# A routed and graph network of eight layers on one core: fifth tile earlier, next matrices into used places, additions between the gelu sums

## The chip, the cores and the metric

The kernel runs on one core of a Trainium2 chip, in one launch. The metric is the time of one execution on the device, in microseconds (us); the time before is the median of three runs.

The core has five engines, each with its own in-order instruction stream: TensorE (PE; PEld is its weight loading), VectorE (DVE), ScalarE (ACT), GpSimd (POOL) and SyncE (SP), which here only issues transfers. They wait for one another on semaphores. TensorE writes into PSUM, eight banks of 512 fp32 values a partition.

## The reference, cut to what matters

`x` has 625 rows of 512 values. Eight layers are added to it one after another, each on a layer-normed `x`; the change touches the third to the seventh.

```
x = x + L0_gnn(ln(x)); x = x + L0_ffn(ln(x))
x = x + L1_gnn(ln(x))     # first graph network in the names below
x = x + L1_ffn(ln(x))     # first expert layer
x = x + L2_gnn(ln(x))     # second graph network, 3 layers
x = x + L2_ffn(ln(x))     # second expert layer
x = x + L3_gnn(ln(x), noise)   # four attention blocks
x = x + L3_ffn(ln(x))     # routed experts
```

The end of L1_gnn, for each row: `h = rowsum @ W1 + b1`, `h = relu(layernorm(h) * gamma + beta)` with 128 values, and `relu(h @ W2 + b2)` with 512, divided by a row weight, is added to `x`.

L2_gnn repeats three times: `agg = CNT @ x`, `y = agg @ Wtop[i] + edge part @ Wbot[i] + bs[i]`, `x = relu(layernorm(x + y) * gamma + beta)`.

L2_ffn is a mixture of 8 experts in which every expert sees every row:

```
top_p = normalized two largest softmax(x @ Wg)
for i in range(2):
    h = gelu((x * top_p[i]) @ W1 + b1)     # 512 x 512 over all experts
    out = out + h @ W2 + sum_e b2
```

L3_gnn begins with a layer norm whose gain and offset are `cond @ s1_w + s1_b` and `cond @ b1_w + b1_b` with 16 values of `cond` a row, made from the noise.

## The kernel before, in words

The 625 rows are five tiles of P = 125 rows (`NT = 5`); `X[:, t, :]` is the residual stream. Each layer is written out by hand for every engine in the order in which it is to be issued; nothing plans it. PSUM is given out by `Slots`: two one-bank slots `T` (turned, that is transposed, rows), two two-bank slots `W` and two one-bank slots `N`. Each engine calls `next` or `skip` in the same sequence; a slot has a semaphore `filled` and one `taken`, and TensorE fills a slot only when what it held two uses before is taken.

**Matrices.** `WR` holds two sets of three 512 x 512 matrices, `wm(s, j)`. `loads` (line 483) is SyncE's program. `load` (line 491) issues a batch after `weights_used` has reached the number of batches that TensorE is through with; TensorE counts it with `weights_done` (line 710), a drain. For the second graph network set 0 holds Wtop of its three layers and set 1 the small Wlast. Behind it, lines 605 to 639, comes the batch of the second expert layer (f_W1, f_W2, f_b2; lines 605 and 498), which waits for the end of the third layer. After it SyncE writes zeros into `x_slots` (4.25 MB, from the cleared tile MODW, lines 618 to 622), waits for their landing, loads eight pieces of modulation weights (modw, line 608), the attention biases (line 612), and the qkv matrices (line 635, issued at line 498).

**First graph network.** Per tile: `hidden_of` (line 1101) makes h in an `N` slot; VectorE's `hidden` (line 2527) adds b1 and takes statistics, POOL takes the inverse root (line 1942), `hidden_normed` (line 2540) normalizes; TensorE turns it (`turn_hidden`, line 1105), ScalarE applies relu; `second` (line 1111) multiplies by W2 in an `N` slot after a product with one row of ones for the bias (line 1113); ScalarE's `second` (line 1747) applies relu; VectorE's `added` (line 2545) adds. VectorE takes tile 4's hidden rows (line 2562) after `added(0)`. Since `N` has two slots, the second product of tile 1 uses the bank that held h of tile 4.

**Second graph network.** Per layer, lines 1168 to 1193: an aggregation of five parts, one for each tile of normed rows, and five narrow products, one for each tile.

**Second expert layer.** TensorE, lines 1215 to 1255: turn each tile, its routing logits (`logit`, into one slot), and its inner projection with f_W1 (tiles 0, 1 and 4 in `N`, line 724; tiles 2 and 3 in one `W` slot, line 1210). Then `modulation(t)` (line 1020), the turn of the gelu sum and `second_of_two(t)` (line 1233: a bias product with eight rows, line 1235, then f_W2, line 1238) for each tile. ScalarE: the five copies of turned rows, rounding of `cond` into CONDR (line 1804), rounding of modw into MODR (`round_weights`, line 1808), the exponential of the routing (`router_exp`, line 1690), then for each tile two gelus (`inner`), the copy of the turned sum and of the modulation. VectorE: the logits' copy and maxima (lines 2680, 2683), the two shares, then the loop at line 2716: two scaled inputs (`hidden_inputs`, line 2696), `split_condition` (line 2706) behind the first tile's and `split_weights` (line 2713) behind the second's, and the sum of the two gelus one tile later (line 2728). When all five sums are made, `three(streamed, stream_normed, modulated_norm)` (line 2783) adds the second products to X (line 2123), normalizes twice and applies the modulation.

Of the kernel before, what the change touches and what calls it, by code (L numbers as in the profile page):

```python
# [21 lines left out]
N, E, D = 625, 10000, 512  # L22
P, NT = 125, 5
# [161 lines left out]
def program(nc, a, out, loops):  # L185
# [11 lines left out]
    def sem(name):  # L197
        return ctx.enter_context(nc.semaphore(name))
# [8 lines left out]
    with ctx:  # L207
# [169 lines left out]
        GE = [[view(PT_ + 512 * (2 * b + i), P, D) for i in range(2)] for b in range(2)]  # L377
        EMN = view(V_ + 1265, 64, N)
# [71 lines left out]
        cond_rounded, cond_split = sem("cond_rounded"), sem("cond_split")  # L450
        mod_rounded, mod_split = sem("mod_rounded"), sem("mod_split")
# [31 lines left out]
        def loads(sp):  # L483
# [121 lines left out]
            load([mat(0, 0, "f_W1"), mat(0, 1, "f_W2"), (WR[0:8, 0, 2, 0:D], a["f_b2"])])  # L605
# [16 lines left out]
            sp.dma_start(x_slots[2048:2048 + 128, :], MODW[:, 0, :]).then_inc(slots_zeroed, 16)  # L622
            sp.wait_ge(slots_zeroed, 16 * 5)
# [71 lines left out]
        def _(pe):  # L695
# [472 lines left out]
            for l in range(3):  # L1168
# [17 lines left out]
                for t in range(NT):  # L1186
                    o = fill("N")
                    mm(o.ap[0:P, :], EA2[0:65, tile(t)], WR[0:65, 1, 1, D * l:D * (l + 1)], start=True, stop=False)
                    for f in range(K4):
                        if t == 0:  # L1190
                            copied(gathered[f])
                        last = mm(o.ap[0:P, :], HT[:, f, tile(t)], wm(0, l)[:, f, :], start=False, stop=(f == K4 - 1))
                    last.then_inc(o.filled, 1)
            weights_done()
# [38 lines left out]
            def second_of_two(t, turned_inner):  # L1233
                s = fill("N")
                mm(s.ap[0:P, :], TWOS[:, :], WR[0:8, 0, 2, 0:D], start=True, stop=False)
                copied(turned_inner)
                for k in range(K4):
                    last = mm(s.ap[0:P, :], HT[:, k, tile(t)], wm(0, 1)[:, k, :], start=False, stop=(k == K4 - 1))
                last.then_inc(s.filled, 1)
# [228 lines left out]
        def _(act):  # L1468
# [334 lines left out]
            transpose_y()  # L1803
            fn(CONDR[:, :], COND4, ACT.Copy).then_inc(cond_rounded, 1)
            def round_weights(j, rows_in_):

                act.wait_ge(rows_in_, n.add(rows_in_, 64))
                fn(MODR[:, :, :], MODW[:, j:j + 2, :], ACT.Copy).then_inc(mod_rounded, 1)
# [10 lines left out]

            round_weights(0, modw_in)  # L1820
# [102 lines left out]
        def _(pool):  # L1923
# [95 lines left out]
            inverse_roots((0, 1, 2, 3, 0, 4, 1, 2, 3, 4))  # L2019
# [53 lines left out]
        def _(dve):  # L2073
# [471 lines left out]
            def added(t):  # L2545
# [12 lines left out]
            fifth = psum.next("N")  # L2558
            seconds = [psum.next("N")[0:2] for t in range(NT)]
            added(0)  # L2560
            dve.wait_ge(fifth[0].filled, fifth[1])
            v.tensor_tensor(HB[:, 4, :], fifth[0].ap[0:P, 0:128], ROWS[:, R_B1:R_B1 + 128], ALU.add)\
             .then_inc(fifth[0].taken, 1)
            dve.wait_ge(fifth[0].taken, fifth[1])
            stats(4, HB[:, 4, :])
            hidden_normed(3)
            added(1)
            norm_y(0)
            hidden_normed(4)
# [108 lines left out]
            psum.skip(T=NT)  # L2678
            s = take("W")
            v.tensor_copy(LG[:, :, :], s.ap[0:P, 0:8 * NT].rearrange("p (t e) -> p t e", t=NT)).then_inc(s.taken, 1)  # L2680
            dve.wait_ge(s.taken, n.now(s.filled))
            for t in range(NT):
                step(v.max(M8[:, t, :], LG[:, t, :]))
            softmax_of_two()
            couple = psum.next("W")

            def hidden_inputs(t):
                if t in (2, 3):
                    s = couple[0]
                    dve.wait_ge(s.filled, couple[1])  # L2690
                    rows = s.ap[0:P, D * (t - 2):D * (t - 1)]
                else:
                    s = take("N")
                    rows = s.ap[0:P, 0:D]
                for i in range(2):
                    last = v.scalar_tensor_tensor(GE[t % 2][i], rows, TW[:, t, 1 + i:2 + i],  # L2696
                                                  ROWS[:, R_FB1:R_FB1 + D], ALU.mult, ALU.add)
                    if i == 0:
                        last.then_inc(negmax_ready, 1)
                last.then_inc(negmax_ready if t == 2 else s.taken, 1)  # L2700

# [14 lines left out]
            for t in range(NT + 1):  # L2716
                if t < NT:
                    if t >= 2:
                        dve.wait_ge(y_ready, n.now(y_ready))
                    hidden_inputs(t)  # L2720
                if t == 0:
                    split_condition()
                if t == 1:
                    split_weights(0)
                if t:
                    dve.wait_ge(exp_ready, n.add(exp_ready, 2))
                    n.add(y_ready)
                    v.tensor_tensor(Y[0:P, t - 1, :], GE[(t - 1) % 2][0], GE[(t - 1) % 2][1], ALU.add)\
                     .then_inc(y_ready, 1)
# [53 lines left out]
            three(streamed, stream_normed, modulated_norm)  # L2783
# [241 lines left out]
```

## Time and profile before

| | |
|---|---|
| median of 3 runs | 2321.89 us |
| lowest, highest | 2321.63, 2322.45 us |
| span of the profiled execution | 2314.6 us (no other time is given for it) |
| TensorE busy | 2155.4 us, 93% |
| VectorE, ScalarE, GpSimd busy | 1043.3, 729.8, 540.3 us |
| chain that ended last | PE 68%, DVE 11%, issue 8%, PEld 4%, ACT 3%, DMA 3%, POOL 3% |

Times in the profile are in us from the start of the span. A row of the timeline is: start, duration, engine, line, operation, what is written from what, shapes, count, and in brackets how long the engine was idle before it and what ended that. In the chain of waits a piece is start, duration and what; "issue" is time in which the engine waited for nothing that the profile shows. In the table of windows the columns are the window, its length, then busy time and number of instructions of PE, PEld, DVE, ACT and POOL, the granted TensorE clock as a share of 2.4 GHz, the share of the DMA engines and GB/s. A busy TensorE is not a TensorE at its peak, and the recorded ends of its products overlap a little with the next.

### The profile page before, as it was taken

Reading aid. Unit: us, or ns where it says so; the run is one execution under the profiler, and the core shown is the slowest. Engines: PE = TensorE matmul, PEld = TensorE weight load, DVE = VectorE, ACT = ScalarE, POOL = GpSimd, SP = SyncE. Lnnn points to the kernel's source line nnn. Section 1 sums busy time; section 2 is a strip of 40 time slices with the busy share of each in tenths; the row PEclk is TensorE's granted clock in tenths of the full one; section 3 lists DMA queues with packets and bytes.
Section 4 is the critical chain, followed back from the end, with each engine's and each line's share of the span. In section 5 each row is a group of like instructions: output and inputs, shape, how many; then the busy total and the mean of one; then the engine's idle time right before and its main releaser. Section 6 shows DMA issues by size and latency. Waiting matters only on the chain.

```text
span 2314.6 us, 21913 instructions
## 1 busy us (share of the span) xinstructions
PE 2155.4 (93%) x8137; PEld 1248.1 (54%) x8137; DVE 1043.3 (45%) x2156; ACT 729.8 (32%) x1221; POOL 540.3 (23%) x457
## 2 busy tenths in 40 slices
PE   6899896888889999988999999999999999999998
PEld 3566563787445555444565565565555544444443
DVE  8897677886324332454454453453453410000002
ACT  1576555675421110003243243243242111111110
POOL 4677762332210000110202202202202200022202
PEclk9999998787999979998999999999999899999999
DMA  9522205431020110023101101101101577787832
GB/s 344 167 31 38 27 4 126 123 78 58 0 96 19 55 55 7 1 76 116 65 9 59 64 10 59 65 10 59 55 1 55 195 272 297 296 306 294 298 143 71
DMA packets 61507, 237.47 MB, mean 103 GB/s; under 512 B 23343, under 2 KB 28419, under 8 KB 39276
## 3 DMA queue, kind: packets, MB, share of 16 engines
q1 hardware_dynamic: 31898, 168.25, 20.3%
q0 software_dynamic: 26336, 62.19, 8.8%
q10 hardware_dynamic: 3168, 5.63, 0.7%
q8 instruction: 66, 1.08, 0.2%
q14 instruction: 39, 0.32, 0.0%
HBM read 204.06 MB, written 31.96 MB: 102 GB/s over the span
## 4 chain that ended last, share of the span: by engine, by line
PE 68%; DVE 11%; issue 8%; PEld 4%; ACT 3%; DMA 3%; POOL 3%; SPq 0%; PEldq 0%; ACTq 0%; DVEq 0%; POOLq 0%
PE PS L996 10%; PE PS L724 10%; PE PS L717 7%; PE PS L1387 7%; PE PS L1396 7%; PE PS L1425 6%; PE PS L868 3%; PE PS L1293 3%; PE PS L1034 2%; PE PS L1273 2%; PE PS L735 1%; DMA pair_scores<-TS,SIDX 1%; PEld PS L717 1%; DVE AR L2406 1%; POOL pair_scores L1971 1%
## 5 line engine op out<-in xcount | busy, mean ns | idle before, releaser
L1942 POOL TENSOR_TENSOR RSTD<-VE,HALF 125x1 f32<-125x1 f32 x100 | 81.7, 817 | 1017.3 <-DVE VE L2101 1017.3
L996 PE MATMUL PS<-XT,WR 128*128 128x500 f32 (+2 forms) x992 | 236.2, 396 | 8.4 <-ACT XT L1493 4.4
L868 PE MATMUL PS<-HR,HOT 125*125 125x512 f32 x800 | 212.8, 414 | 16.4 <-DVE HOT L2245 16.4
L724 PE MATMUL PS<-WR,XT 128*125 128x512 f32 (+1 forms) x464 | 208.0, 596 | 12.2 <-DVE AR L2696 7.7
L2911 DVE TENSOR_TENSOR AR<-AR,PS 128x512 f32<-128x512 f32 (+1 forms) x44 | 30.2, 687 | 404.9 <-PE PS L1396 404.9
L996 PEld LDWEIGHTS PS<-XT,WR 128*128 128x128 f32 x992 | 146.0, 194 | 89.2 <-issue 74.7
L868 PEld LDWEIGHTS PS<-HR,HOT 125*125 125x125 f32 x800 | 147.9, 193 | 58.5 <-DVE HOT L2245 16.8
L1960 POOL DMA_INDIRECT pair_sums<-CW,SIDX x80 | 136.2, 1703 | 56.3 <-DMA pair_sums<-CW,SIDX 24.5
L724 PEld LDWEIGHTS PS<-WR,XT 128*125 128x125 f32 x464 | 87.1, 194 | 101.4 <-issue 86.4
L717 PE MATMUL PS<-XT,WR 128*128 128x113 f32 (+3 forms) x432 | 127.5, 453 | 1.8 <-DVE CW L2209 1.3
L1902 ACT ACTIVATE AR<-PS 128x512 f32<-128x512 f32 (+1 forms) x44 | 26.3, 597 | 299.3 <-PE PS L1387 299.3
L2123 DVE TENSOR_TENSOR AR<-PS,AR 125x512 f32<-125x512 f32 x55 | 38.0, 691 | 178.7 <-PE PS L724 106.3
L717 PEld LDWEIGHTS PS<-XT,WR 128*128 128x128 f32 (+1 forms) x432 | 69.8, 196 | 65.3 <-issue 64.1
L1971 POOL DMA_INDIRECT pair_scores<-TS,SIDX x80 | 89.1, 1114 | 61.4 <-DMA pair_scores<-TS,SIDX 46.5
L1493 ACT ACTIVATE XT<-PS 128x500 f32<-128x500 f32 x60 | 35.4, 590 | 214.0 <-PE PS L735 214.0
L717 PE MATMUL PS<-AR 128*125 128x113 f32 (+3 forms) x360 | 102.4, 439 | 0.0
L1425 PE MATMUL PS<-AR,MODW 128*128 128x512 f32 (+1 forms) x192 | 86.4, 593 | 0.7 <-ACT MODW L1891 0.7
L1994 POOL TENSOR_TENSOR AR<-AR,CNT 125x625 f32<-125x625 f32 x40 | 56.8, 1419 | 104.9 <-ACT AR L1658 104.9
L717 PEld LDWEIGHTS PS<-AR 128*125 128x125 f32 (+1 forms) x360 | 57.3, 187 | 43.8 <-issue 43.6
L724 PE MATMUL PS<-WR,AR 128*125 128x512 f32 (+1 forms) x200 | 76.6, 530 | 1.7 <-ACT AR L1876 0.9
L2245 DVE SCALAR_TENSOR_TENSOR HOT<-AR,NODE,WR 125x500 fp32r<-125x500 int16 x100 | 71.2, 731 | 7.0 <-ACT WR L1525 6.0
L2266 DVE TENSOR_REDUCE TS<-WR 125x8 f32<-125x512 f32 x80 | 54.4, 680 | 42.1 <-DMA pair_scores<-TS,SIDX 42.1
(422 smaller groups left out, 3940.3 us busy)
## 6 DMA issues: line engine op xcount, KB each, us to landing
WR<-in_qkv SPq DMA_DIRECT2D x12, 1024.0 KB
WR<-in_omm SPq DMA_DIRECT2D x12, 1024.0 KB
pair_scores<-CNT SPq DMA_DIRECT2D x1, 12212.0 KB, 36.4
AR<-pair_scores SPq DMA_DIRECT2D x5, 2187.5 KB
AR<-in_x_a SPq DMA_DIRECT2D x10, 1024.0 KB, 9.8
AR<-in_x_b SPq DMA_DIRECT2D x10, 1024.0 KB, 4.9
AR<-in_x_c SPq DMA_DIRECT2D x10, 1024.0 KB, 7.2
WR<-in_x_a SPq DMA_DIRECT2D x8, 1024.0 KB, 8.9
```

What stands on the lines that cost most here:

```text
L717: last = mm(s.ap[0:parts, c0:c1], lhs(k), rhs(k)[:, c0:c1], start=(k == 0), stop=(k == terms - 1))
L724: last = mm(s.ap[0:P, 0:cols], lhs, rhs, start=(k == 0), stop=(k == len(pairs) - 1))
L868: last = mm(DIFF[m % 4], HOT[g % 2][0:P, k, tile(j)], HR[0:P, k, :, b, :], start=(k == 0 and b == 0), stop=(k == NT - 1 and b == 1))
L996: last = mm(by_tile(s)[:, t0:t1, :], w[:, k, 128 * m:128 * (m + 1)], XT[:, k, P * t0:P * t1].rearrange("p (c n) -> p c n", n=P), start=(k ...
L1293: one = mm(main.ap[:, 0:MAIN], v_, PTH[h % 2][:, k, 0:MAIN], start=(k == 0), stop=(k == NT - 1))
L1387: last = mm(bank(2 + k % 2, rows_of(k)), stationary(k, c), w[:, c, :], start=(c == 0), stop=(c == K4 - 1))
L1396: last = mm(bank(4 + k % 2, rows_of(k)), stationary(k, c), w[:, c, :], start=(c == 0), stop=(c == K4 - 1))
L1425: last = mm(bank(6 + n % 2, rows), HTX[k % 2][:, c, 0:rows], w[:, c, :], start=(u == 0 and c == 0), stop=((is_shared(k) or u == 1) and c = ...
L1942: g.tensor_tensor(RSTD[:, t:t + 1], VE[:, t:t + 1], HALF[:, :], ALU.pow)\
L1960: g.indirect_dma_start(out=pair_sums[m % 2], out_offset=bass.IndirectOffsetOnAxis(ap=SIDX[:, m:m + 1], axis=0), in_=CW[:, m, :], in_offset ...
L1971: g.indirect_dma_start(out=pair_scores, out_offset=bass.IndirectOffsetOnAxis(ap=SIDX[:, m:m + 1], axis=0), in_=TS[:, m % SCORES_AHEAD, :], ...
L2245: v.scalar_tensor_tensor(HOT[g % 2][0:P, k, :], IDB[g // 2 % 2][0:P, 1, 500 * (g % 2):500 * (g % 2 + 1)], NODE[:, 0, k:k + 1], FROM[q % 4] ...
```

## The change

Four edits go together. VectorE's tile 4 of the hidden rows is taken and normalized before the first addition, and POOL's roots follow that order. f_W1 and f_W2 are loaded singly into the places of Wtop 0 and Wtop 1 when TensorE is through with the layer that used them (a drain with a semaphore behind layers 0 and 1), f_b2 into a new place `OUTER_BIAS`, all behind the zeroing of `x_slots`, which so stands at the start of the second graph network. ScalarE rounds `cond` before the five turned copies instead of behind them, and VectorE splits it before the logits. VectorE's first addition of a second product stands before the last gelu sum instead of behind it; the rest of `three` is written out in the same order.

```diff
+        OUTER_BIAS = view(PT_ + 2340, 8, D)
+        graph_layer_done = sem("graph_layer_done")
@@ SyncE
-            load([mat(0, 0, "f_W1"), mat(0, 1, "f_W2"), (WR[0:8, 0, 2, 0:D], a["f_b2"])])
...
             sp.dma_start(x_slots[2048:2048 + 128, :], MODW[:, 0, :]).then_inc(slots_zeroed, 16)
+            k2 = batch[0]
+            batch[0] += 1
+            for l, (dst, src) in enumerate((mat(0, 0, "f_W1"), mat(0, 1, "f_W2"), (OUTER_BIAS, a["f_b2"]))):
+                if l < 2:
+                    sp.wait_ge(graph_layer_done, l + 1)
+                sp.dma_start(dst, src).then_inc(loaded[k2 % 2], 16)
+                landed[k2 % 2] += 16
             sp.wait_ge(slots_zeroed, 16 * 5)
@@ TensorE, behind each layer l of the second graph network
+                if l < 2:
+                    pe.drain().then_inc(graph_layer_done, 1)
...
-                mm(s.ap[0:P, :], TWOS[:, :], WR[0:8, 0, 2, 0:D], start=True, stop=False)
+                mm(s.ap[0:P, :], TWOS[:, :], OUTER_BIAS, start=True, stop=False)
@@ ScalarE
-            transpose_y()
             fn(CONDR[:, :], COND4, ACT.Copy).then_inc(cond_rounded, 1)
...
+            transpose_y()
             round_weights(0, modw_in)
@@ POOL
-            inverse_roots((0, 1, 2, 3, 0, 4, 1, 2, 3, 4))
+            inverse_roots((0, 1, 2, 3, 4, 0, 1, 2, 3, 4))
@@ VectorE, first graph network
             hidden(3)
             hidden_normed(2)
-            fifth = psum.next("N")
+            hidden(4)
+            hidden_normed(3)
+            hidden_normed(4)
             seconds = [psum.next("N")[0:2] for t in range(NT)]
             added(0)
-            dve.wait_ge(fifth[0].filled, fifth[1])
-            v.tensor_tensor(HB[:, 4, :], fifth[0].ap[0:P, 0:128], ROWS[:, R_B1:R_B1 + 128], ALU.add)\
-             .then_inc(fifth[0].taken, 1)
-            dve.wait_ge(fifth[0].taken, fifth[1])
-            stats(4, HB[:, 4, :])
-            hidden_normed(3)
             added(1)
             norm_y(0)
-            hidden_normed(4)
@@ VectorE, second expert layer
+            split_condition()
             psum.skip(T=NT)
             s = take("W")
...
+            inner_at = {t: psum.next("N") for t in (0, 1, 4)}
+            seconds = [psum.next("N") for t in range(NT)]
...
+            def second_streamed(t):
+                s, k = seconds[t][0:2]
+                dve.wait_ge(s.filled, k)
+                v.tensor_tensor(X[0:P, t, :], s.ap[0:P, :], X[0:P, t, :], ALU.add).then_inc(s.taken, 1)
+                dve.wait_ge(s.taken, k)
+                stats(t, X[0:P, t, :])
...
-            three(streamed, stream_normed, modulated_norm)
+            for t in range(NT + 1):
+                if t < NT:
+                    if t >= 2:
+                        dve.wait_ge(y_ready, n.now(y_ready))
+                    hidden_inputs(t)
+                if t == 1:
+                    split_weights(0)
+                if t == NT:
+                    second_streamed(0)
+                if t:
+                    inner_sum(t - 1)
+            for t in range(1, NT + 2):
+                if t < NT:
+                    second_streamed(t)
+                if t <= NT:
+                    stream_normed(t - 1)
+                if t >= 2:
+                    modulated_norm(t - 2)
```

## Rows read from the trace of the kernel before

**Rows 1.** The chain of waits, 1018 to 1130 us: start, us, what.
```profile
1031.66 15.82 DMA x_slots<-MODW
...
1048.43 12.51 DMA MODW<-in_modw
...
1060.96 1.06 ACT MODR L1808
...
1062.04 1.28 ACT L1692
...
1063.33 0.22 ACT TW L1692
```

**Rows 2.** SyncE's timeline, issues between 820 and 1112 us.
```profile
1028.46 0.80 SPq L498 DMA_DIRECT2D WR<-in_f_W  x2
...
1058.39 6.12 SPq L498 DMA_DIRECT2D WR<-in_qkv  x3
```

**Rows 3.** TensorE's timeline in the second expert layer.
```profile
1032.25 0.94 PE L1202 MATMUL PS<-WG,XT 128*125 128x8 f32 x8
1037.39 5.44 PE L724 MATMUL PS<-WR,XT 128*125 128x512 f32 x8 [4.20 <-DMA WR<-in_f_b]
...
1043.89 3.68 PE L724 MATMUL PS<-WR,XT 128*125 128x512 f32 x8
...
1052.14 0.59 PE L735 MATMUL PS<-CS,Y 125*128 125x125 f32 x4
...
1065.67 6.65 PE L724 MATMUL PS<-WR,XT 128*125 128x512 f32 x8 [7.69 <-DVE AR L2696]
...
1087.88 1.28 PE L1235 MATMUL PS<-WR,TWOS 8*125 8x512 f32 x2 [3.11 <-DVE X L2123]
1089.09 5.19 PE L1238 MATMUL PS<-WR,AR 128*125 128x512 f32 x8
```

**Rows 4.** VectorE's timeline in the second expert layer.
```profile
1036.60 0.54 DVE L2106 TENSOR_SCALAR Y<-X,MV,RSTD 125x512 f32<-125x512 f32 x1
...
1054.49 0.20 DVE L2680 COPY LG<-PS 125x40 f32<-125x40 f32 x1 [12.60 <-PE PS L1202]
...
1055.74 0.17 DVE L2603 TENSOR_TENSOR TW<-M 125x5 f32<-125x5 f32 x1
...
1064.21 1.41 DVE L2696 SCALAR_TENSOR_TENSOR AR<-PS,TW,AR 125x512 f32<-125x512 f32 x2
1065.65 1.62 DVE L2706 TENSOR_TENSOR CONDR<-AR,CONDR 32x625 fp32r<-32x625 f32 x2
...
1072.05 0.68 DVE L2728 TENSOR_TENSOR Y<-AR 125x512 f32<-125x512 f32 x1
...
1080.96 0.69 DVE L2728 TENSOR_TENSOR Y<-AR 125x512 f32<-125x512 f32 x1 [3.38 <-ACT AR L1796]
1086.53 0.69 DVE L2728 TENSOR_TENSOR Y<-AR 125x512 f32<-125x512 f32 x1 [4.88 <-ACT AR L1796]
```

**Rows 5.** Timelines of TensorE and VectorE, hidden rows of the first graph network.
```profile
799.33 0.35 DVE L2538 SCALAR_TENSOR_TENSOR AR<-AR,RSTD 125x128 f32<-125x128 f32 x1
...
804.36 0.28 DVE L2562 TENSOR_TENSOR AR<-PS,AR 125x128 f32<-125x128 f32 x1
...
804.70 2.06 PE L1113 MATMUL PS<-AR,ONES 1*125 1x512 f32 x2 [2.73 <-DVE AR L2562]
```

**Rows 6.** Table of windows: length, busy times, granted clock, DMA share, GB/s.
```profile
792.00:801.90 9.90, 9.75 (x55) 6.40 (x55) 5.35 (x22) 1.99 (x5) 2.30 (x4) 1.00 0.00 0
802.00:804.70 2.70, 0.00 (x0) 0.00 (x1) 1.94 (x6) 0.75 (x2) 0.17 (x1) 0.50 0.00 0
804.70:822.00 17.30, 17.30 (x22) 5.21 (x22) 8.37 (x22) 2.98 (x6) 3.30 (x5) 0.50 0.00 1
...
1072.00:1088.00 16.00, 12.89 (x44) 6.39 (x43) 6.37 (x11) 8.27 (x16) 0.00 (x0) 1.00 0.12 47
```

**Rows 7.** TensorE's timeline behind the drain that ends the first expert layer.
```profile
898.77 11.06 PE L1174 MATMUL PS<-CNT,AR 125*128 125x512 f32 x40 [0.26 <-issue]
```

More of the change, by code:

```diff
@@ L2675, in _ @@
             three(summed, lambda t: relu_normed(t, 2), norm_y)
[L2678 to L2700, printed above, removed]
             def split_condition():
@@ L2714, in split_weights @@
                                 MODR[64:128, :, :].bitcast(F32), ALU.subtract).then_inc(mod_split, 1)
[L2716 to L2729, printed above, removed]
+            split_condition()
@@ new lines, in _ @@
+            psum.skip(T=NT)
+            s = take("W")
+            v.tensor_copy(LG[:, :, :], s.ap[0:P, 0:8 * NT].rearrange("p (t e) -> p t e", t=NT)).then_inc(s.taken, 1)
+            dve.wait_ge(s.taken, n.now(s.filled))
+            for t in range(NT):
+                step(v.max(M8[:, t, :], LG[:, t, :]))
+            softmax_of_two()
+            couple = psum.next("W")
+            inner_at = {t: psum.next("N") for t in (0, 1, 4)}
+            seconds = [psum.next("N") for t in range(NT)]
@@ new lines, in hidden_inputs @@
+            def hidden_inputs(t):
+                if t in (2, 3):
+                    s, k = couple[0:2]
+                    rows = s.ap[0:P, D * (t - 2):D * (t - 1)]
+                else:
+                    s, k = inner_at[t][0:2]
+                    rows = s.ap[0:P, 0:D]
+                dve.wait_ge(s.filled, k)
+                for i in range(2):
+                    last = v.scalar_tensor_tensor(GE[t % 2][i], rows, TW[:, t, 1 + i:2 + i],
+                                                  ROWS[:, R_FB1:R_FB1 + D], ALU.mult, ALU.add)
+                    if i == 0:
+                        last.then_inc(negmax_ready, 1)
+                last.then_inc(negmax_ready if t == 2 else s.taken, 1)
@@ new lines, in inner_sum @@
+            def inner_sum(t):
+                dve.wait_ge(exp_ready, n.add(exp_ready, 2))
+                n.add(y_ready)
+                v.tensor_tensor(Y[0:P, t, :], GE[t % 2][0], GE[t % 2][1], ALU.add).then_inc(y_ready, 1)
+            def second_streamed(t):
+                s, k = seconds[t][0:2]
+                dve.wait_ge(s.filled, k)
+                v.tensor_tensor(X[0:P, t, :], s.ap[0:P, :], X[0:P, t, :], ALU.add).then_inc(s.taken, 1)
+                dve.wait_ge(s.taken, k)
+                stats(t, X[0:P, t, :])
```

## The prediction

> **What bounds the kernel now.** TensorE is busy almost everywhere, so I read the chain of waits first and looked for the pieces of it that are not TensorE. Around the second expert layer it holds two transfers and what hangs on them: 15.82 us in which the slots in memory are zeroed, then 12.51 us for the rows of the modulation weights (modw), then ScalarE's rounding of those rows, and behind it, in the same in-order engine, the exponential of the routing softmax [rows 1]. SyncE's queue shows why: it waits for the end of the second graph network before it issues f_W1 and f_W2 at 1028.46, the zeroing and the modw rows stand behind them, and the qkv weights get out only at 1058.39 [rows 2]. TensorE's timeline shows the price: 4.20 us idle for the transfer of f_b2 that closes the f batch, a projection of tile 4 that starts only at 1065.67 and takes 6.65 us where one at full clock takes 3.68, and 3.11 us idle in front of the third second product [rows 3]. One other place is touched, the hidden rows of the first graph network: 2.73 us idle for the bank of the fifth tile [rows 5]. The windows give TensorE's clock there [rows 6].
>
> **Part 1, fifth tile in front of the first addition.** VectorE now reads tile 4 out of its bank at 804.36, behind `added(0)`, though it was through with the normalization of tile 2 at 799.7 [rows 5]. The same reading then comes at about 799.7 to 800.0, and the bank is free before TensorE asks for it at 804.70 - 2.73 = 801.97. The statistics and two normalizations that come with it fill VectorE's idle time up to `added(0)`, which waits for ScalarE in both kernels. The reordered roots on POOL only follow VectorE's order. So the 2.73 us idle goes: **-2.7 us**. What is late next is TensorE itself: from 804.7 to 822 it is busy 17.30 of 17.30 us, at 1.2 GHz [rows 6]. That clock decides the size. It was full up to 801.9, during 9.75 us busy of 9.90, and half from 802.0 on, so it had gone down as the idle time began, not behind it, and 17 us of unbroken work (products with one row of ones, alternating with the W2 products) did not bring it back [rows 6]. What runs before 801.9 is unchanged, so I let the clock fall again. Lower end of the gain 2.0, upper 11.4 (rival A).
>
> The Trainium skill, "TensorE: Matmul & The Clock Gate", Part 1 and its list for kernel authors, holds that idle time throttles the array and work releases it. By that the removed stall would also give back the slow stretch behind it. The rows here speak against it, since the fall comes with no idle time ahead of it; it is rival A.
>
> **Part 2, the next matrices into used places.** Added: a drain of TensorE behind layers 0 and 1 of the second graph network. The trace has no drain inside those layers; the nearest is the one ahead of 898.77, with 0.26 us idle [rows 7]. Bounds 0.2 and 0.6 each, since weight loading can't run ahead over it either; I take 0.4, **+0.8 us** for both. VectorE's last normalization of a layer is asked for only by the last of the five parts of the next aggregation, so nothing else waits.
>
> Moved on SyncE's queue: the five zeroing transfers go right behind Wlast and the clearing of MODW, at the start of this network, where no other transfer is queued; then f_W1 after layer 0, f_W2 and f_b2 (to a new place, since its old one still holds layer 2's matrix) after layer 1, and, as the zeroing has long landed, the eight modw transfers and the attention biases. All of it comes some 40 us before layer 2 ends. The qkv load waits only for that end and issues near 1028.5 instead of 1058.39 [rows 2]; it is not needed before 1095. The queue is never late: even 13 us for the modw rows, as before [rows 1], end before 1000.
>
> What that gives, step by step. The first projection starts when the first routing logits are done, at 1032.25 + 0.94 = 1033.2, instead of 1037.39 [rows 3]. Full speed would end it at 1036.9; since TensorE has just stood idle I let half of it run at 1.2 GHz: 1038.4. Tile 2's normed rows are there at 1037.14 [rows 4], no longer the last to come. Before, from the start of the first projection to the fourth turn (1037.39 to 1052.14) it took 14.75 us; that contains 5.44 for the first projection, so 9.3 behind it, plus the 0.3 us or so of pipelining: turn of tile 4 at 1048.1 [rows 3]. From that turn to the copy of the logits VectorE needed 1054.49 - 1052.14 = 2.35 [rows 3, 4]: 1050.4. The maxima and the difference end 1.42 later (1054.49 to 1055.91 [rows 4]): 1051.9. Here, before, ScalarE stood at the modw rows and exponentiated at 1063.33 [rows 1]; now rounding (1.06) and table load (1.28) [rows 1] start at about 1049.4, end with the difference, and the exponential runs at once. From it to the first hidden input it is 1064.21 - 1063.33 = 0.9 [rows 1, 4]: 1052.8 against 1064.21, **11.4 us earlier**: 4.1 from the f weights, 7.3 from the modw rows. The projection of tile 4 follows 1.46 later (1065.67 - 1064.21), at 1054.3, with TensorE idle for under 1 us instead of 7.7, so at full clock: 3.68 instead of 6.65, end 1057.9 against 1072.3. That is 14.4.
>
> What is late next: the second gelu sum. It ended at 1072.05 + 0.68, 8.52 behind the first hidden input; `split_condition` (1.62 us of VectorE between the two [rows 4]) is moved ahead of the logits, where VectorE idled for 12 us, and ScalarE's copy for it to before the turns: 6.9. So it ends at 1059.7, where TensorE would turn that tile at 58.8: 0.9 back. **-13.5 us** for the part; if the first projection runs at full clock -15.2, if the clock stays low for one more projection -10.
>
> **Part 3, additions between the gelu sums.** The third second product waits until `streamed(0)` has emptied its bank, and VectorE does that only behind the last gelu sum, which itself waited for ScalarE until 1086.53 [rows 4]. Now it stands in front of that sum: right behind the fourth (1080.96 + 0.69 = 1081.65 [rows 4]), 3 us before TensorE asks at 1087.88 - 3.11 = 1084.77 [rows 3]. So 3.11 idle goes, and with it the slow clock behind it: 5.19 against 3.68, and some 0.2 in the bias product ahead of it, 4.8 in all. The next bank is freed by the addition of tile 1, right behind the last sum at 87.2, in time. I give back 0.2 since the first modulated rows of tile 0 come out level with TensorE's turn of them. VectorE's tail behind the last product is the same work. **-4.6 us**; bounds -3 (VectorE late) and -4.8.
>
> Sum: -2.7 + 0.8 - 13.5 - 4.6 = **-20.0 us**. The profiled execution has a span of 2314.6; the page gives no separate time for it, and the median of 2321.89 lies 7.3 above the span, which I carry over unchanged. 2321.9 - 20.0 = **2301.9 us**. Everything behind the layer is shifted as it is; only the clock's falls and returns in it may land elsewhere, for which I allow 2 us either way.
>
> **Rivals.**
> A: the clock stays at 2.4 GHz in the hidden rows. For: the stall that is removed stands at the head of the slow stretch. Against: the fall came with none ahead of it [rows 6]. Price: half of 17.3 us, 8.7 more gain: **2293.2**. Chance 0.13.
> B: the clock stays low from the first f projection to that of tile 4. For: in the hidden rows busy TensorE stayed at 1.2 GHz. Against: in the kernel before the same projections took 5.44 and then 3.68, so it returned inside one [rows 3], and 1072 to 1088 ran at 1.00 [rows 6]. Price: four projections of 3.68 doubled, 14.7: gain 5.3, **2316.6**. Chance 0.06.
> C, the other side: with nothing waited for any more, the mixture of eight-row bias products, turns and ten groups of 3.68 keeps TensorE at 1.2 GHz through the whole layer. Price 10 x 3.68 = 36.8 against 20.0: **2338.7**, slower; it decides from more than five of the ten groups at half clock. For: as B, and 1-row products did it at 804.7. Against: rows 6 again. Chance 0.02.
> D: the early transfers change nothing, because something else holds the exponential (the turn of tile 4 is late). Then only parts 1 and 3 and the end of the cold projection stay, about 9 us: **2313**. Against: ScalarE's only recorded wait there is for modw [rows 1]. Chance 0.05.
>
> **How the numbers follow.** Forecast 0.74; A, B, C, D as given. The forecast's own range is 2297 to 2307. To leave out no more than 2 in 10 with its ends and A's uncertain place, the range is 2291 to 2309. A difference of 0.2% (4.6 us) is about what can be told from none here. Faster by more than that: all but C and a sliver of B and D: 0.97; within 0.01; slower 0.02.
>
> **What would show it.** No idle at L1113 and its pair still near 4.1 us: part 1 as forecast; at 2.1 us, A. The zeroing within the first layer of the second graph network, an f matrix behind each of the first two layers, qkv at the end of the third: the queue. MODR rounded by ScalarE directly behind the last turn's copy, and 3.7 us for all narrow projections but the first: part 2. No idle over 0.5 us at L1235: part 3. Gaps above 1 us behind layers 0 and 1 would refute the price of the drains. A total above 2309 would mean that a wait which I have not seen replaced the modw rows.

## The result and the profile after

The changed kernel took 2298.51 us (median of 4, 2295.84 to 2299.26) against 2321.76 before (median of 4); the ratio is 0.9908 with a 95% interval of 0.9884 to 0.9932, that is 16 to 27 us less. The profiled execution had a span of 2293.7 us, 20.9 less than before.

| | before | after |
|---|---|---|
| median | 2321.76 | 2298.51 |
| span of the profiled execution | 2314.6 | 2293.7 |
| TensorE busy | 2155.4, 93% | 2152.0, 94% |
| VectorE, ScalarE, GpSimd busy | 1043.3, 729.8, 540.3 | 1043.4, 729.8, 537.8 |

The work is the same; what went is time in which TensorE waited, or worked at 1.2 GHz. The change adds and moves lines. TensorE's L743 is the old L735 (turns), L732 the old L724, L1121 and L1123 the old L1113 and L1115, L1212 the old L1202, L1245 and L1248 the old L1235 and L1238. VectorE's L2701 is the old L2680 (copy of the logits), L2609 the old L2603, L2719 the old L2696 (hidden inputs), L2688 the old L2706 (split of `cond`); the gelu sum has L2728 in both.

SyncE's timeline of the changed kernel (it answers [rows 2]):

```profile
895.06 0.33 SPq L500 DMA_DIRECT2D WR<-in_Wlast  x1
900.46 3.06 SPq L621 DMA_DIRECT2D x_slots<-MODW  x4
...
938.69 43.96 SPq L629 DMA_DIRECT2D WR<-in_f_W  x2
982.68 0.33 SPq L629 DMA_DIRECT2D AR<-in_f_b  x1
983.06 6.76 SPq L609 DMA_DIRECT2D MODW<-in_modw  x8
...
1026.06 1.30 SPq L500 DMA_DIRECT2D WR<-in_qkv  x3
...
1084.59 1.28 SPq L500 DMA_DIRECT2D WR<-in_omm  x3
```

The zeroing goes out at 900.5, f_W1 after the first layer, f_W2, f_b2 and the modulation rows after the second, qkv at 1026, the end of the third. Before, all of these were issued between 1028.5 and 1058.4. (A duration such as 43.96 contains the wait between the first and the last of the merged issues.)

ScalarE's and VectorE's timelines in the second expert layer (they answer [rows 1, 4]):

```profile
1046.31 1.05 ACT L1818 ACTIVATE MODR<-MODW 128x1024 fp32r<-128x1024 f32 x1
1047.38 1.28 ACT L1702 ACT_TABLE_LOAD   x1
1049.00 0.21 ACT L1702 ACTIVATE TW<-TW 125x5 f32<-125x5 f32 x1 [0.34 <-DVE TW L2609]
```

```profile
1034.08 0.54 DVE L2117 TENSOR_SCALAR Y<-X,MV,RSTD 125x512 f32<-125x512 f32 x1
...
1039.40 1.62 DVE L2688 TENSOR_TENSOR CONDR<-AR,CONDR 32x625 fp32r<-32x625 f32 x2
1047.55 0.20 DVE L2701 COPY LG<-PS 125x40 f32<-125x40 f32 x1 [6.53 <-PE PS L1212]
...
1048.80 0.17 DVE L2609 TENSOR_TENSOR TW<-M 125x5 f32<-125x5 f32 x1
...
1049.89 2.73 DVE L2719 SCALAR_TENSOR_TENSOR AR<-PS,TW,AR 125x512 f32<-125x512 f32 x4
...
1055.95 0.68 DVE L2728 TENSOR_TENSOR Y<-AR 125x512 f32<-125x512 f32 x1
...
1064.72 0.69 DVE L2728 TENSOR_TENSOR Y<-AR 125x512 f32<-125x512 f32 x1 [4.41 <-ACT AR L1806]
1065.33 0.68 DVE L2733 TENSOR_TENSOR X<-PS,X 125x512 f32<-125x512 f32 x1
...
1070.29 0.69 DVE L2728 TENSOR_TENSOR Y<-AR 125x512 f32<-125x512 f32 x1 [3.14 <-ACT AR L1806]
```

ScalarE rounds the modulation rows directly behind its last copy and loads its table, and the exponential waits 0.34 us for VectorE, not 7 us for a transfer. The split of `cond` fills idle time ahead of the logits. The first addition (1065.33) stands between the fourth gelu sum (1064.72) and the last (1070.29).

TensorE's timeline there (it answers [rows 3]):

```profile
1029.72 1.13 PE L1212 MATMUL PS<-WG,XT 128*125 128x8 f32 x8
1030.71 5.18 PE L732 MATMUL PS<-WR,XT 128*125 128x512 f32 x8
...
1036.95 3.68 PE L732 MATMUL PS<-WR,XT 128*125 128x512 f32 x8
...
1045.20 0.59 PE L743 MATMUL PS<-CS,Y 125*128 125x125 f32 x4
...
1051.35 3.70 PE L732 MATMUL PS<-WR,XT 128*125 128x512 f32 x8 [0.31 <-DVE AR L2719]
...
1056.78 0.62 PE L743 MATMUL PS<-CS,Y 125*128 125x125 f32 x4 [0.84 <-DVE Y L2728]
...
1068.46 1.12 PE L1245 MATMUL PS<-AR,TWOS 8*125 8x512 f32 x2
1069.51 3.70 PE L1248 MATMUL PS<-WR,AR 128*125 128x512 f32 x8
```

The first projection follows the logits at once, and is slow (5.18 for 3.68) as it was before; the projection of tile 4 takes 3.70 instead of 6.65; a new wait of 0.84 stands at the second turned sum (L743 at 1056.78); and no idle time is left at L1245, and the product behind it (L1248) takes 3.70 instead of 5.19.

TensorE's timeline and the table of windows at the hidden rows of the first graph network ([rows 5, 6]), and TensorE's timeline behind the first new drain ([rows 7]):

```profile
801.52 1.98 PE L1121 MATMUL PS<-AR,ONES 1*125 1x512 f32 x2
803.43 2.07 PE L1123 MATMUL PS<-WR,AR 128*125 128x512 f32 x2
```

```profile
791.70:801.50 9.80, 9.73 (x55) 6.40 (x55) 7.37 (x30) 1.90 (x5) 2.89 (x5) 1.00 0.00 0
801.60:819.00 17.40, 17.14 (x22) 5.13 (x23) 8.25 (x19) 3.97 (x9) 2.89 (x4) 0.50 0.00 0
...
1051.00:1088.00 37.00, 32.98 (x97) 15.06 (x96) 27.48 (x56) 14.19 (x27) 6.19 (x8) 1.00 0.06 22
```

```profile
938.87 11.06 PE L1182 MATMUL PS<-CNT,AR 125*128 125x512 f32 x40 [0.26 <-issue]
```

The stall of 2.73 is gone. What follows is as before: 17.14 us busy of 17.40, at 1.2 GHz. The clock is low from the second pair of products on, though TensorE was busy 9.73 of the 9.80 us ahead of it and nothing stalls in between.

### A measure that is finer than the runs

Executions of the same kernel differed by up to 18 us (58 runs of the kernel before: 2310.23 to 2328.71), and most of that seems to arise ahead of 770 us, where the change does nothing: the first product of the aggregation in the first graph network started between 763.2 and 777.2 in the 14 profiles. From there on profiles of the same code agree to a fraction of a microsecond, except where TensorE's clock falls or returns at another product (1.3 to 1.7 us at a time in the table), so each kernel is read between landmarks, all starts of TensorE instructions: A that aggregation (L1092 before), B the first aggregation of the second graph network, C the first turn behind it, D the first modulation of the second expert layer, E the first bias product there (L1235 before), F the first product of the attention blocks (L996 at 1112.42 before). One profile each, in us:

| kernel | A to B | B to C | C to D | D to E | E to F | F to end |
|---|---|---|---|---|---|---|
| before | 129.20 | 129.99 | 43.00 | 1.81 | 38.85 | 1202.18 |
| changed | 126.06 | 130.98 | 28.25 | 2.85 | 34.19 | 1202.18 |
| e1 fifth only | 124.74 | 129.99 | 41.55 | 3.18 | 42.06 | 1202.71 |
| e2 transfers only | 129.04 | 130.99 | 29.94 | 2.84 | 41.97 | 1202.62 |
| e3 additions only | 129.13 | 129.99 | 42.84 | 2.03 | 34.17 | 1202.63 |
| e4 bias 125 rows | 114.51 | 130.98 | 28.27 | 2.84 | 34.17 | 1202.72 |
| e5 no drains | 126.02 | 130.02 | 28.23 | 2.84 | 35.88 | 1201.76 |
| e6 zeroing late | 126.13 | 131.00 | 35.35 | 1.82 | 34.19 | 1202.68 |
| e7 f late | 126.04 | 130.99 | 31.39 | 2.83 | 34.17 | 1202.33 |
| e9 before, bias 125 | 116.49 | 129.99 | 42.72 | 2.35 | 40.31 | 1202.72 |
| e10, e12 best | 114.51, 114.51 | 129.99, 129.99 | 29.56, 29.56 | 2.84, 2.84 | 34.17, 34.16 | 1202.47, 1202.52 |
| e11, e13 changed | 126.04, 124.73 | 130.98, 131.01 | 28.24, 28.26 | 2.84, 2.84 | 34.17, 34.17 | 1202.21, 1202.78 |

Changed against before: part 1 (A to B) -3.14, drains (B to C) +0.99, transfers (C to E) -14.75 + 1.04, additions (E to F) -4.66: -20.5 in all.

### The profile page after: what moved, and what is told of

It is laid out like the page before. It is cut to its first block, busy times and chain, and to the rows that moved or that the text cites. A ratio compares the mean times of both kernels' runs of the same rounds, so it can differ in the third digit from the quotient of the medians.

```text
span 2293.7 us, 21915 instructions
## 1 busy us (share of the span) xinstructions
PE 2152.0 (94%) x8137; PEld 1248.6 (54%) x8137; DVE 1043.4 (45%) x2156; ACT 729.8 (32%) x1221; POOL 537.8 (23%) x457
## 4 chain that ended last, share of the span: by engine, by line
PE 76%; DVE 11%; issue 4%; POOL 3%; ACT 3%; DMA 2%; ACTq 0%; DVEq 0%; POOLq 0%
PE PS L732 10%; PE PS L1004 10%; PE PS L725 9%; PE PS L1397 7%; PE PS L1406 7%; PE PS L1435 6%; PE PS L876 3%; PE PS L1303 3%; PE PS L1042 3%; PE PS L1283 2%; PE PS L1200 2%; PE PS L743 1%; PE PS L1182 1%; DMA pair_scores<-TS,SIDX 1%; DVE AR L2417 1%
## 5 line engine op out<-in xcount | busy, mean ns | idle before, releaser
L876 PE MATMUL PS<-HR,HOT 125*125 125x512 f32 x800 | 212.5, 414 | 15.2 <-DVE HOT L2256 15.2
L732 PE MATMUL PS<-WR,XT 128*125 128x512 f32 (+1 forms) x464 | 205.3, 590 | 0.6 <-DVE AR L2719 0.3
L732 PEld LDWEIGHTS PS<-WR,XT 128*125 128x125 f32 x464 | 86.6, 193 | 87.9 <-issue 84.6
L732 PE MATMUL PS<-WR,AR 128*125 128x512 f32 (+1 forms) x200 | 76.6, 530 | 1.7 <-ACT AR L1887 0.9
```

What stands on the lines that cost most here:

```text
L732: last = mm(s.ap[0:P, 0:cols], lhs, rhs, start=(k == 0), stop=(k == len(pairs) - 1))
L876: last = mm(DIFF[m % 4], HOT[g % 2][0:P, k, tile(j)], HR[0:P, k, :, b, :], start=(k == 0 and b == 0), stop=(k == NT - 1 and b == 1))
```

## The experiments

### e1, e2, e3: one part at a time

The three kernels are the kernel before with the diff's edits of one part each; e2 has the transfers, the drains and the earlier rounding and splitting of `cond`.

> Part 1 alone on the kernel before: tile 4 of the hidden rows in front of the first addition. Theory (the step is the 2.73 us of idle TensorE and nothing else): no idle at L1113, its product pairs still some 4.1 us apart at 1.2 GHz, the two turns behind the stage 2.7 to 2.9 us earlier than before, the whole 2.5 to 3.5 us shorter. Rival A (the stall had brought the clock down): pairs of 2.1 us and 8 to 12 us shorter. Rival 'hidden': something behind it (VectorE's first addition, ScalarE) takes the place of the stall and it is under 1 us.

Measured: ratio 0.9983 (0.9969 to 0.9996), 0.9 to 7 us less. No idle at L1113, pairs of 4.1 us; A to B 4.5 less. The size of the step is the stall of 2.73 and up to 1.7 us from where the clock falls and returns around it: the clock falls within the first W2 product (1.46 us for 1.12), but the first product behind the stretch is at full clock again, 2.76 us where it took 4.87 in the profile of before. TensorE's timeline of e1:

```profile
828.68 2.76 PE L996 MATMUL PS<-XT,WR 128*128 128x375 f32 x8 [0.88 <-ACT XT L1703]
```

In another profile of the changed kernel (e13) A to B is 124.73 as well; in the five others with part 1 and the one-row product it is 126.0 to 126.1. Rival A is out. So is "hidden".

> Part 2 alone on the kernel before: next matrices into used places, zeroing and modulation rows ahead, cond rounded and split earlier. Theory: the first hidden input of the second expert layer 11 to 12 us earlier, the modulation of tile 0 about 14.5, minus 0.9 at the second turned sum, minus 0.9 for two drains: 12.5 to 14.5 us shorter in all, with the idle in front of the third second product (3.1 us) still there. Rival (the three parts need one another, a wait of part 3 hides part of the gain): under 10 us.

Measured: ratio 0.994 (0.9916 to 0.9963), 9 to 20 us less. C to D 13.1 less, D to E 1.0 more, B to C 1.0 more. C to D gains 1.7 less than in the changed kernel, since the first projection took 6.71 us here and 5.18 there. The idle at the third second product is still there, and it costs more than in the profile of before: TensorE's timeline of e2,

```profile
1035.46 6.71 PE L732 MATMUL PS<-WR,XT 128*125 128x512 f32 x8
...
1064.66 5.40 PE L1248 MATMUL PS<-WR,AR 128*125 128x512 f32 x8
...
1079.63 2.06 PE L1245 MATMUL PS<-AR,TWOS 8*125 8x512 f32 x2 [3.11 <-DVE X L2134]
1081.62 5.83 PE L1248 MATMUL PS<-WR,AR 128*125 128x512 f32 x8
```

has 2.06 for the bias product and 5.83 for the one behind it, where [rows 3] have 1.28 and 5.19: 1.4 us more. E to F is 3.1 longer than in the profile of before; the other 1.7 lies ahead of the stall, in the second product of the first tile (5.40 at 1064.66, where it took 3.70 before). e1 has both as well (5.39 for that product, 42.06 in all), with the edits of part 1 only.

> Part 3 alone on the kernel before: the first addition of a second product stands in front of the last gelu sum. Theory: the 3.11 us idle at L1235 gone and the product behind it 3.7 instead of 5.2 us, 4.4 to 4.8 us shorter. Rival (VectorE, one addition later at each step, is late with the modulated rows of tile 0): 2 to 3 us shorter and a new idle of 1 to 2 us ahead of the turn of those rows.

Measured: ratio 0.9985 (0.9965 to 1.0006), by the times alone inconclusive. E to F is 34.17, 4.7 less than in the profile of before and 7.8 less than in e1 and e2. No new idle ahead of the turn of tile 0's rows. All kernels with part 3 show 34.2, but for 35.88 in e5, where the second product of the first tile ran slow (5.40), as it did in e1 and e2. That 1.7 us therefore comes and goes without the stall, and part 3 is not shown to remove it. Without it the stretch with the stall is 38.85 (before), 40.3 (e1, e2) and 40.31 (e9), so the stall costs 4.7 us once and 6.1 three times.

The three times add to 3.9 + 13.9 + 3.5 = 21.3 us, against 21.4 (ratio 0.9908 of 2321.76) for all together. The intervals of the three add up to some 8 us either way, so this alone says little. Between the landmarks that each part touches the three give -4.5, -11.0 and -4.7, 20.2 together for the 20.5 of the changed kernel: no part is seen to need another.

### e5, e6, e7: what in part 2 carries the gain

These are edits of the changed kernel, with one timed execution each (2293.63, 2303.3 and 2292.95 us); between executions that can be 18 us apart such a time says little, so they are read by the landmarks.

e5 takes the drains out and lets SyncE wait for VectorE's count, which can't be reached before TensorE is through with the layer:

```diff
-                    sp.wait_ge(graph_layer_done, l + 1)
+                    sp.wait_ge(layer_ready, 14 + NT * (l + 1))
...
-                if l < 2:
-                    pe.drain().then_inc(graph_layer_done, 1)
```

> The changed kernel without its two drains: SyncE waits for VectorE's count of normalized tiles (tile 4 of layers 0 and 1) before f_W1 and f_W2 instead. Theory (the drains are the whole price of part 2 on TensorE): from the first aggregation of the second graph network to its last product 129.99 us as in the kernel before, not 130.98; the f matrices issued some 5 us later, with nothing behind them changed. Rival (the extra microsecond is contention of the early transfers with TensorE or with VectorE): it stays at about 131.0.

Measured: B to C 130.02. The drains are the whole microsecond, 0.5 each, though the idle recorded behind each is 0.26. The rest is weight loading, which does not run ahead over the drain. The rows of PEld for the first weights behind layer 0, in the changed kernel and in e5:

```profile
938.84 0.30 PEld L1182 LDWEIGHTS PS<-CNT,AR 125*128 125x128 f32 x2 [1.06 <-issue]
```

```profile
935.64 0.19 PEld L1182 LDWEIGHTS PS<-CNT,AR 125*128 125x128 f32 x1 [0.24 <-issue]
```

Behind the drain the load starts 0.03 us ahead of its product (938.87), after 1.06 us without a load; in e5 it starts 0.43 ahead (936.07), after the usual 0.24. No contention of the early transfers is to be seen.

e6 leaves f_W1, f_W2 and f_b2 early and puts the zeroing and all behind it back:

```diff
+            sp.wait_ge(weights_used, 7)
             sp.wait_ge(mod_split, 1)
             for q in range(4):
```

(these lines and the zeroing now stand behind the three f loads.)

> The changed kernel with only f_W1, f_W2 and f_b2 early; zeroing of the slots, modulation rows, attention biases and qkv again behind the end of the second graph network. Theory (the modulation rows hold ScalarE's rounding and with it the exponential): zeroing alone takes 10 to 11 us, the modulation rows 12.5 more, so the routing exponential comes 4 to 6 us later than in the changed kernel, TensorE idles 4 us or more ahead of the projection of tile 4, which runs at 1.2 GHz: 6 to 9 us longer than the changed kernel. Rival D (something else holds the exponential): within 1 us of the changed kernel.

Measured: C to E 6.1 longer than in the changed kernel. SyncE's, ScalarE's and TensorE's timelines of e6:

```profile
1026.86 3.06 SPq L629 DMA_DIRECT2D x_slots<-MODW  x4
...
1038.93 5.01 SPq L609 DMA_DIRECT2D MODW<-in_modw  x8
```

```profile
1052.26 1.06 ACT L1819 ACTIVATE MODR<-MODW 128x1024 fp32r<-128x1024 f32 x1 [4.93 <-DMA MODW<-in_modw]
...
1054.63 0.21 ACT L1703 ACTIVATE TW<-TW 125x5 f32<-125x5 f32 x1
```

```profile
1056.98 6.10 PE L733 MATMUL PS<-WR,XT 128*125 128x512 f32 x8 [5.02 <-DVE AR L2720]
```

The modulation rows hold the rounding, and the exponential is 4.7 later from C (27.5 for 22.8). Rival D is out. The modulation rows land 13.3 us behind their issue at 1038.93, and that issue waited 12 us for the zeroing. Issued at 1026.9 themselves they would have landed near 1040 by the same duration (an estimate), ahead of the 1047.3 at which ScalarE began to wait; but MODW, into which they are loaded, is also the source of the zeros. So neither the zeroing nor the rows alone hold ScalarE here, but the one behind the other does; no run delays only one of them.

e7 leaves zeroing and modulation rows early and loads the f batch behind the end of the third layer:

```diff
                 attention_biases(i)
+                if i == 0:
+                    load([mat(0, 0, "f_W1"), mat(0, 1, "f_W2"), (OUTER_BIAS, a["f_b2"])])
```

> The changed kernel with the f batch again behind the end of the second graph network, ahead of qkv; zeroing and modulation rows stay early. Theory: the f batch has the transfer engines for itself and lands 7 us after its issue instead of 8.7, so the first projection starts 2 to 3 us later than in the changed kernel and the layer is 2 to 4 us longer. Rival (the early f matrices are worth nothing, since tile 2's normed rows come 6.7 us after tile 0's turn anyway): under 1 us. Rival (the f matrices carry most of the gain): over 6 us.

TensorE's timeline of e7:

```profile
1027.57 5.40 PE L727 MATMUL PS<-WR,XT 128*125 128x512 f32 x8 [2.69 <-DMA AR<-in_f_b]
```

Measured: 2.69 us idle for f_b2, C to D 3.14 longer than in the changed kernel. So of the 14.75 us the f matrices alone carry 3.1 and the zeroing with the modulation rows 7.1. The other 4.5 appear only when both are late. With the f batch in front, the modulation rows are issued 18.7 behind C (before) instead of 11.8 (e6), and the exponential comes 34.6 behind C instead of 27.5; the first projection starts 8.6 behind C (before) instead of 7.4 (e7). How the 4.5 divide over these, and what of them is only where the clock returns (tile 4's projection took 6.65 before, 6.10 in e6, 5.14 in e1), is not separated.

### e4, e9: the slow clock of the hidden rows

One edit, to the changed kernel in e4 and to the kernel before in e9. The identity times 125 equal rows is the same sum as one row of ones times one row:

```diff
-                mm(s.ap[0:P, :], ONES[0:1, 0:P], ROWS[0:1, R_B2:R_B2 + D], start=True, stop=False)
+                mm(s.ap[0:P, :], ID[0:P, 0:P], ROWS[0:P, R_B2:R_B2 + D], start=True, stop=False)
```

> The changed kernel with one edit: the bias product of the hidden rows (first graph network) multiplies the identity by all 125 equal rows of the bias instead of one row of ones by one row; same columns, same result. Theory (the slow clock in this stretch hangs on how few rows the bias products use, not on idle time): the pairs fall from 4.1 to 2.1 us, the stretch is 8 to 11 us shorter than in the changed kernel, so 29 to 34 us shorter than the kernel before. Rival (the clock had gone down for the idle times and narrow products before it and only long unbroken work of one kind brings it back): pairs stay at 4.1 us, no difference from the changed kernel (21 to 23 us shorter than before).

Measured: ratio 0.9874 (0.9835 to 0.9912), and A to B 11.5 us shorter than in the changed kernel (10.2 against e13). TensorE's timeline of e4:

```profile
806.15 1.02 PE L1121 MATMUL PS<-AR,CS 125*125 125x512 f32 x2
807.01 1.02 PE L1123 MATMUL PS<-WR,AR 128*125 128x512 f32 x2
...
815.60 0.62 PE L743 MATMUL PS<-CS,Y 125*128 125x125 f32 x4 [0.88 <-DVE Y L2117]
817.09 2.76 PE L1004 MATMUL PS<-XT,WR 128*128 128x375 f32 x8 [0.88 <-ACT XT L1713]
```

Both products of a pair take 1.02 us, at 2.4 GHz, from the second pair to the last; the stretch is then short enough that VectorE's normed rows are late by 0.88, and the first product behind it takes 2.76 instead of 4.6, as it does in e1 and e13 without this edit. Not all of the gain is clock. At full clock, before, the pair with one row had these starts:

```profile
799.69 1.12 PE L1113 MATMUL PS<-AR,ONES 1*125 1x512 f32 x2
800.74 1.12 PE L1115 MATMUL PS<-WR,AR 128*125 128x512 f32 x2
```

The one-row products hold TensorE 1.05 us from start to start, the 125-row ones 0.86 (806.15 to 807.01). Over the four pairs of the stretch that is some 0.8 of the 11.5 us, an estimate.

> The kernel before with one edit: the bias product of the hidden rows uses the identity and 125 equal rows. The 2.73 us stall for tile 4 stays. Theory (few rows hold the clock down, a stall alone of this length does not): the stall is still there, the pairs behind it at 2.1 us, or at 4.1 us for the first one or two at most; the stretch 6 to 9 us shorter than in the kernel before. Rival (the stall has a part in the fall): clock low behind the stall for most of the stretch, under 4 us.

Measured: ratio 0.9954 (0.9939 to 0.9969), A to B 12.7 shorter than before. TensorE's timeline of e9:

```profile
802.35 1.14 PE L1113 MATMUL PS<-AR,CS 125*125 125x512 f32 x2 [2.73 <-DVE AR L2562]
803.31 1.88 PE L1115 MATMUL PS<-WR,AR 128*125 128x512 f32 x2
...
805.20 1.79 PE L1113 MATMUL PS<-AR,CS 125*125 125x512 f32 x2
806.83 1.02 PE L1115 MATMUL PS<-WR,AR 128*125 128x512 f32 x2
809.03 0.30 PE L1108 MATMUL PS<-CS,AR 125*128 125x125 f32 x1 [1.18 <-DVE AR L2538]
```

The stall of 2.73 is there. The bias product right behind it takes 1.14, the two that follow run slow (1.88 and 1.79), and then it is 1.02 again. So a stall of this length can cost two slow products, but it is the one-row products that hold TensorE at 1.2 GHz. Only 1, 8 and 125 rows were tried, the 8 in another mixture, and the edit changes both operands, so neither a limit in rows nor which operand counts is shown. More was gained than either theory said (6 to 9, under 4). Up to the first product behind the stretch it is 7.3, as the first theory has it. That product is faster by 2.1 (4.87 to 2.76), and the other 3.3 come in the first expert layer, where the granted clock was 0.85 over 44 us before and 0.92 over 41 us in e9: where the clock falls there differs from profile to profile. With full clock part 1 is worth 2.0 from A to B (116.49 to 114.51): 5.3 up to the first product behind the stretch, of which 3.3 are lost again in that expert layer (granted clock 0.85 in e4).

### e10 to e13: the version that the runs point to

e10 and e12 are the changed kernel with e4's and e5's edits, e11 and e13 the changed kernel itself.

> The changed kernel with both edits that the runs so far point to: identity and 125 equal rows in the bias product of the hidden rows (11.5 us between landmarks), and SyncE waiting for VectorE's count instead of two drains (1.0 us). If they add up: 12 to 13 us shorter than the changed kernel, 33 to 37 us shorter than the kernel before. If the clock's falls and returns further on eat part of it: 8 to 11 us shorter than the changed kernel.

> The changed kernel as it is, on the same chip as the last version, for a narrower interval. Theory (the three parts add up as measured between landmarks, part 3 worth 4.7 to 7.8 us with the clock's phase): 20 to 24 us shorter than the kernel before. If the first comparison was lucky: 17 to 20.

Measured: e10 0.9856 (0.9836 to 0.9875), 2288.89 us; e11 0.9871 (0.9851 to 0.9891), 2294.32 us, so 30 us less than the 2323.41 of before on that chip, more than expected. From A to the end e10 took 10.9 less than e11, but its median was only 5.4 lower, which is under both of the ranges expected for it (12 to 13, 8 to 11).

> The version with the 125-row bias product and no drains once more, beside the changed kernel on one chip. From the landmark of the first aggregation of the first graph network to the end it took 10.9 us less than the changed kernel, but its median lay only 5.4 us below. Theory (the stretch ahead of that landmark, which the edits don't touch, differs by up to 12 us between executions, and five or six draws of it are too few): the landmark difference is again 10 to 12 us, and the medians of all runs taken together come nearer to it, 6 to 12 us. Rival (the edits make that earlier stretch slower): the landmark lies later in this version again, by 3 us or more, and the medians stay under 6 us apart.

> The changed kernel once more, as the other half of that comparison: landmark to end 1524 to 1525 us as in both profiles so far; ratio to the kernel before between 0.988 and 0.992, that is 19 to 28 us shorter.

Measured: e12 0.9857 (0.9826 to 0.9889), 2287.52 us; e13 0.9911 (0.9878 to 0.9943), 2297.36 us. Over all runs, on several chips: before 2321.97 (58 runs), changed 2297.04 (16), this version 2288.55 (11): 24.9 and 33.4 us less than before. From A to the end this version takes 1513.5 and 1513.6 against 1523.8 to 1524.5, 10.2 to 11.0 apart (C to D is 1.3 longer in it: the logits ahead of the first projection take 1.69 us for 1.13 and it takes 5.51 for 5.18). Landmark A lay at 773.3 and 777.2 in it, at 772.7 and 767.6 in the changed kernel beside it: 0.6 and 9.6 later. The medians are 8.5 apart. The theory holds for what follows A; whether the 2 us that are missing in the medians are draws or something that the edits do ahead of A is not settled by three or four profiles.

## Why the prediction was right

- **Part 1** (forecast -2.7): -3.14 in the profile, -4.5 in e1 and e13. The stall went, the slow pairs stayed. The added 0.4 to 1.7 is the clock returning earlier against the work: 4.62 and 2.76 us for the first product behind the stretch, which took 4.87 before.
- **Rival A** did not come, and its price of 8.7 was too small: e4 gained 11.5 there. 9.5 of it lie in the stretch itself (17.48 us from the first one-row product after the fall to the turn behind the stretch, 7.95 in e4), where the 125-row products are also shorter by themselves, and 1.9 in the first product behind it. The Trainium skill's rule, idle time throttles and work releases ("TensorE: Matmul & The Clock Gate", Part 1 and its list for kernel authors), does not describe this stretch: 17.14 us of work in 17.40 us left the clock where it was. The rows decide.
- **Drains** (forecast +0.8): +1.0, shown by e5, inside the bounds, and the reason given for more than the idle holds there too.
- **Part 2**: turn of tile 4 at C + 19.0 (forecast 1048.1 - 1028.76 = 19.3), first hidden input at C + 23.7 (forecast 24.0), first modulation 14.75 earlier (forecast 14.4), late second sum 1.04 (forecast 0.9). In all -13.7 for -13.5. The first projection was slow for the part that was assumed (5.18), and there luck had a hand: where the clock returns differs between profiles, and in e2 it took 6.71, with a granted clock of 0.54 over it, which made the whole part 1.7 us smaller. The sum has a slip of 0.3 in it: half of 3.68 at half clock ends at 1038.7, not 1038.4. By the sum's own numbers a first projection at full clock gives -15.0, not -15.2. The split "4.1 from the f weights, 7.3 from the modulation rows" holds for the second, 7.1 in e6; for the first e7 gives 3.1. The two were taken as adding up; with only one of them late they give 10.2 of the 14.75, and 4.5 need both.
- **Part 3** (forecast -4.6): -4.66 against the profile of before. That it came so close is in part luck too: as the price of the stall in general it was too small: that profile caught a cheap case, and in e1, e2 and e9 the stall cost 6.1, with two products behind it slow for longer.
- **The step that failed** is the carry from the span to the median. "7.3 above the span, which I carry over unchanged" was not a constant: in every profiled execution whose own time is known the time is 2.0 to 2.1 above the span, so the execution profiled before took near 2316.7, an estimate, some 5 under the median. The profile of before was thus a short execution, and part of what made it short was a cost that part 3 removes: the stall took 1.4 less there than in e1, e2 and e9. Span against span the sum was -20.0 for a measured -20.9 (-20.5 from A on); against the medians it was 3.4 too small (2301.9 for 2298.51), and 4.9 against the medians of all runs.
- **Rivals B and C** did not come: 3.7 for every projection but the first, and granted clock 1.00 over the 37 us from 1051 to 1088. Eight-row bias products among 125-row ones do not bring it down.

## What to carry to other kernels

Look in a single in-order transfer queue for what stands behind a wait that it doesn't need: here one wait for the end of a layer held a zeroing of 4.25 MB, and behind it small rows that ScalarE needed first, and the two in a row carried 7.1 us of the gain against 3.1 for the matrices that TensorE needs (each group late alone). Where TensorE is 100% busy at half clock, look at how many rows its products use before looking for idle time: in this stretch a bias product of one row was replaced by one of 125 rows with the same number of columns, and the clock stayed at 2.4 GHz. And where executions differ by more than the change, compare distances between landmarks inside the profiles.

## What the hardware showed that I had not expected

- A product of one row by 512 columns is no shorter than one of 125 rows (1.12 against 1.02 us at 2.4 GHz, from start to start 1.05 against 0.86), and a sequence in which every second product has one row stays at 1.2 GHz through 17.14 us of work in 17.40 us; with 125 rows the same sequence ran at 2.4 GHz throughout (e4).
- A stall of 3.11 us cost 4.7 or 6.1 us in all, depending on where in the products behind it the clock fell and returned (bias product 1.28 or 2.06, the next 5.19 or 5.83 to 5.91).
- A drain of TensorE between two unbroken stretches cost 0.5 us, about twice the idle time recorded for it (0.26), since the next weights are loaded only behind it.
